# Longer loop bodies and an earlier first front in the two axis stages of a convolution and state-space kernel

## What is computed

```python
def selective_scan(u, delta, A, B, C, D):
    A = jnp.clip(A, -5.0, 5.0)
    dA = jnp.einsum('bld,dn->bldn', delta, A)
    dB_u = jnp.einsum('bld,bld,bln->bldn', delta, u, B)
    c = jnp.concatenate([dA[:, 1:], jnp.zeros_like(dA[:, :1])], axis=1)
    c = jnp.exp(jnp.minimum(jnp.cumsum(jnp.flip(c, axis=1), axis=1), 15.0))
    c = jnp.flip(c, axis=1)
    x = jnp.cumsum(dB_u * c, axis=1) / (c + 1e-06)
    y = jnp.einsum('bldn,bln->bld', x, C)
    return y + u * D

def mamba(x, in_w, conv_w, conv_b, xproj_w, dproj_w, dproj_b, A_log, Dp, out_w):
    ...   # in-projection, 4-tap convolution over the sequence, SiLU
    A = -jnp.exp(jnp.clip(A_log, -5.0, 5.0))
    ...   # delta, B, C from the projection of x1
    y = selective_scan(x1, delta, A, B, C, Dp)
    return y * jax.nn.silu(res) @ out_w.T
```

## Time and profile before

| what | value |
|---|---|
| runs | 19094.44, 19100.8, 19101.3 us |
| the profiled execution, its own time | 19113.85 us |
| span of the profile, first to last instruction | 19112.1 us |
| PE busy | 16120.1 us (84%) |
| VectorE busy | 17478.0 us (91%) |
| ScalarE busy | 13984.3 us (73%) |
| GpSimd busy | 15672.6 us (82%) |
| mean granted TensorE clock | 0.964 |

### The profile page before, as it was taken

How to read it: one execution, slowest core, us unless ns; L and a number is a source line. 1 busy time by engine, 2 the same in 40 slices (tenths; PEclk the granted TensorE clock), 3 DMA queues, 4 the chain that set the end, 5 groups by cost and what they waited for, 6 DMA issues and landing times. The chain is left out here.

```text
span 19112.1 us, 290534 instructions
## 1 busy us (share of the span) xinstructions
PE 16120.1 (84%) x60280; PEld 8249.4 (43%) x60280; DVE 17478.0 (91%) x48304; ACT 13984.3 (73%) x18454; POOL 15672.6 (82%) x10820
## 2 busy tenths in 40 slices
PE   5786888888888888888688888888888888887666
PEld 2333444444444444444344444444444444442222
DVE  3888999999999999999899999999999999996666
ACT  4665777777777777777577777777777777772566
POOL 2665888888888889888699999999999999984555
PEclk8998999999999999999899999999999999998888
DMA  1001000000000000000000000000000000000000
GB/s 33 14 13 14 11 11 10 10 10 11 11 11 11 11 11 11 11 11 11 12 11 11 11 11 11 11 11 11 11 11 11 11 11 11 11 9 22 11 11 10
DMA packets 778298, 228.57 MB, mean 12 GB/s; under 512 B 747760, under 2 KB 750476, under 8 KB 776332
## 3 DMA queue, kind: packets, MB, share of 16 engines
q1 hardware_dynamic: 776332, 206.79, 8.3%
HBM read 143.66 MB, written 62.97 MB: 11 GB/s over the span
## 5 line engine op out<-in xcount | busy, mean ns | idle before, releaser
L1238 POOL TENSOR_TENSOR h_sm<-h_sm,h_wr 128x768 f32<-128x768 f32 x2944 | 5399.7, 1834 | 695.6 <-DVE h_wr L1018 610.2
L1238 POOL TENSOR_TENSOR w_sm<-w_sm,w_wr 128x768 f32<-128x768 f32 x2944 | 5398.5, 1834 | 502.5 <-DVE w_wr L1018 405.0
L1402 PE MATMUL w_pz<-w_xr,w_tri 128*128 128x384 f32 x9984 | 4461.3, 530 | 787.3 <-DVE w_wr L1018 620.9
L1402 PE MATMUL h_pz<-h_xr,h_tri 128*128 128x384 f32 x9984 | 4436.6, 527 | 767.6 <-DVE h_wr L1018 603.5
L1018 DVE SCALAR_TENSOR_TENSOR h_wr<-h_pz,h_bct,h_rbuf 128x192 f32<-128x192 f32 x11776 | 4253.3, 408 | 181.3 <-PE h_pz L1402 180.8
L1018 DVE SCALAR_TENSOR_TENSOR w_wr<-w_pz,w_bct,w_rbuf 128x192 f32<-128x192 f32 x11776 | 4242.2, 408 | 99.2 <-PE w_pz L1402 98.7
L992 DVE SCALAR_TENSOR_TENSOR h_xr<-h_cbuf,h_bct,h_pdx 128x192 f32<-128x192 f32 x9984 | 3635.8, 405 | 73.5 <-issue 32.9
L992 DVE SCALAR_TENSOR_TENSOR w_xr<-w_cbuf,w_bct,w_pdx 128x192 f32<-128x192 f32 x9984 | 3634.5, 405 | 74.1 <-issue 33.1
L1114 ACT ACTIVATE h_cbuf<-h_pe_e,h_consts 128x1024 f32<-128x1024 f32 x2304 | 2525.7, 1112 | 1541.6 <-PE h_pe_e L1390 1341.2
L1114 ACT ACTIVATE w_cbuf<-w_pe_e,w_consts 128x1024 f32<-128x1024 f32 x2304 | 2526.4, 1112 | 1493.9 <-PE w_pe_e L1390 1295.8
L1137 ACT ACTIVATE w_rbuf<-w_pe_e,w_consts 128x1024 f32<-128x1024 f32 x2304 | 2476.3, 1113 | 0.0
(11 more groups left out here) (362 smaller groups left out, 20130.6 us busy)
## 6 DMA issues: line engine op xcount, KB each, us to landing
h_lt<-pieces_s SPq DMA_DIRECT2D x512, 96.0 KB, 4.4
w_lt<-pieces_s SPq DMA_DIRECT2D x512, 96.0 KB, 4.3
pieces_s<-h_pieces SPq DMA_DIRECT2D x384, 48.0 KB, 2.1
pieces_s<-w_pieces SPq DMA_DIRECT2D x384, 48.0 KB, 2.1
h_xt<-first_s SPq DMA_DIRECT2D x34, 128.0 KB, 5.5
w_xt<-first_s SPq DMA_DIRECT2D x34, 128.0 KB, 3.1
m_u<-hn_s SPq DMA_DIRECT2D x32, 128.8 KB, 2.7
m_u<-slots_s SPq DMA_DIRECT2D x32, 128.8 KB, 2.6
```

The source lines that it names most:

```text
L1238: tt(sm[:, g], sm[:, g], wr[:, u % 3], ALU.add).then_inc(s_add, 1)
L1402: t.matmul(pz[:, P % 2, 0:2 * DX], tri[:], x, start=True, stop=True).then_inc(s_z, 1)
```

## The change

Three things change, all in `phase_axis`.

1. The loop's body holds six passes instead of two (`BODY`): 10 turns for passes 1 to 60, and passes 61, 62 and 63 written out.
2. The weight loads are split over two queues: 15 stay on SyncE, 12 are issued by ScalarE. The first input load moves from behind `s_go` to behind the clearing of `xt` (new semaphore `s_pad`), which now is the first of the memsets.
3. `s_go` is given ahead of the pieces of A and the spreading. The clip of A moves to the front of VectorE's preparation (`s_clip`). Of the 16 spreading instructions VectorE issues 7 (3 before the prefix sum, 4 behind it), ScalarE 6 (ahead of its first `c_group`) and GpSimd 3 (behind its third piece); TensorE waits for the three of them (`s_dec`) before the first `fill`.

```diff
+        BODY = 6
+        TURNS = (NT2 - 2) // BODY
@@ bodies
-            with eng.Fori(0, NT2 // 2 - 1) as m:
-                for k in (1, 2):
-                    yield m * 2 + k, k % 2, m + 1, False, False
-            yield NT2 - 1, 1, 0, False, True
+            with eng.Fori(0, TURNS) as m:
+                for k in range(1, BODY + 1):
+                    yield m * BODY + k, k % 2, m * (BODY // 2) + (k + 1) // 2, False, False
+            for T in range(TURNS * BODY + 1, NT2):
+                yield T, T % 2, (T + 1) // 2, False, T == NT2 - 1
@@ sync
+                sp.wait_ge(s_pad, 1)
+                load_x(place(0), 0)
                 sp.wait_ge(s_go, 1)
-                load_x(place(0), 0)
@@ vector
-                for big in (inw, inz, wdt, wbc, wo, xt):
+                v.memset(xt[:], 0.0).then_inc(s_pad, 1)
+                for big in (inw, inz, wdt, wbc, wo):
                     v.memset(big[:], 0.0)
...
                 dve.wait_ge(s_w, 16 * NW)
+                v.tensor_scalar(am, am, -5.0, 5.0, ALU.max, ALU.min).then_inc(s_clip, 1)
...
-                for d in range(16):
-                    last = v.tensor_scalar(decay[:, :, :, d], asel.rearrange("p (m n) -> p m n", n=NX), low4[:, d:d + 1],
-                                           None, ALU.mult)
-                step(last)
                 for m, (s, n) in enumerate([(s_r, 2), (s_wd, 2), (s_add, UN), (s_res, 1), (s_e, 2 * GRP), (s_go, 1)]):
                     v.memset(mark[:, m:m + 1], 0.0).then_inc(s, n)
...
+                a_pieces()
                 make_xc(0, 0)
+                for d in range(3):
+                    make_decay(d)
                 prefix(0)
+                for d in range(3, 7):
+                    last = make_decay(d)
+                last.then_inc(s_dec, 1)
                 make_gate(0, 0)
@@ scalar
+                act.wait_ge(s_asel, 1)
                 piece1(0)
                 piece2(0)
                 sig_z(3)
+                for d in range(10, 16):
+                    last = a.activation(decay[:, :, :, d], asel.rearrange("p (m n) -> p m n", n=NX), ACT.Identity,
+                                        scale=low4[:, d:d + 1])
+                last.then_inc(s_dec, 1)
@@ gpsimd
                 piece3(0)
+                for d in range(7, 10):
+                    last = nc.gpsimd.tensor_scalar(decay[:, :, :, d], asel.rearrange("p (m n) -> p m n", n=NX),
+                                                   low4[:, d:d + 1], None, ALU.mult)
+                last.then_inc(s_dec, 1)
@@ tensor
                 pe.wait_ge(s_lt[0], 128)
+                pe.wait_ge(s_dec, 3)
```

More of the change, by code:

```diff
@@ L769, in phase_axis @@
         s_go, s_xt, s_pd = sem(tag + "prepared"), sem(tag + "input"), sem(tag + "pieces_stored")
+        s_pad, s_clip, s_asel, s_dec = (sem(tag + n) for n in ("input_cleared", "a_clipped", "a_pieces", "decay_made"))
         s_lt = [sem(tag + "pieces_loaded0"), sem(tag + "pieces_loaded1")]
@@ L836, in _ @@
                 ld(ident[:], ident_in)
[L837 to L840, removed]
                 for i in range(8):
@@ L942, in _, with a_pieces, make_decay @@
                 step(v.tensor_tensor(bsc[:, 1:2], bn[:, 1:2], bsc[:, 2:3], ALU.subtract))
[L944 to L954, removed]
-                for d in range(16):
-                    last = v.tensor_scalar(decay[:, :, :, d], asel.rearrange("p (m n) -> p m n", n=NX), low4[:, d:d + 1],
-                                           None, ALU.mult)
-                step(last)
                 for m, (s, n) in enumerate([(s_r, 2), (s_wd, 2), (s_add, UN), (s_res, 1), (s_e, 2 * GRP), (s_go, 1)]):
                     v.memset(mark[:, m:m + 1], 0.0).then_inc(s, n)
+                def a_pieces():
+                    dve.wait_ge(s_aexp, 2)
+                    step(v.tensor_scalar(am, am, 5.0, None, ALU.min))
+                    step(v.tensor_copy(around, am))
+                    v.tensor_scalar(asel, around, pick[:, 0:1], None, ALU.mult)
+                    step(v.tensor_tensor(arest, am, around, ALU.subtract))
+                    step(v.tensor_copy(around, arest))
+                    v.scalar_tensor_tensor(asel, around, pick[:, 1:2], asel, ALU.mult, ALU.add)
+                    step(v.tensor_tensor(arest, arest, around, ALU.subtract))
+                    step(v.tensor_copy(around, arest))
+                    v.scalar_tensor_tensor(asel, around, pick[:, 2:3], asel, ALU.mult, ALU.add).then_inc(s_asel, 1)
+                    dve.wait_ge(s_asel, 1)
+                def make_decay(d):
+                    return v.tensor_scalar(decay[:, :, :, d], asel.rearrange("p (m n) -> p m n", n=NX),
+                                           low4[:, d:d + 1], None, ALU.mult)
                 def make_xc(F, q):
@@ L1054, in _, with ld @@
                 a = nc.scalar
+                def ld(dst, src):
+                    act.dma_start(dst, src).then_inc(s_w, 16)
+                ld(inT, w["inT"])
+                ld(upT, w["upT"])
+                ld(dtT, w["dtT"])
+                ld(taps, w["taps"].rearrange("k (j d) -> k j d", j=JB).partition_broadcast(128))
+                for g in range(2):
+                    q = slice(64 * g, 64 * g + 64)
+                    ld(down2[:, q], w["down"])
+                    ld(outw2[:, :, g, :], w["outw"].rearrange("e (j d) -> e j d", j=JB))
+                    ld(xpr2[:, :, g, :], w["xpr"].rearrange("r (j d) -> r j d", j=JB))
+                    ld(xpT[q], w["xpT"].rearrange("(j d) n -> d j n", j=JB))
                 act.wait_ge(s_prep, 1)
@@ L1059, in _ @@
                 a.activation(bsc[:, 3:4], bsc[:, 3:4], ACT.Exp, scale=-0.5).then_inc(s_aexp, 1)
-                act.wait_ge(s_aexp, 2)
+                act.wait_ge(s_clip, 1)
                 a.activation(am, am, ACT.Exp).then_inc(s_aexp, 1)
```

4 lines of the change are left out of this document (removed).

## The result

The changed kernel takes **18935.2 us** in the median of four runs. Before took 19101.05 us on the same chip. The ratio of the undisturbed runs is 0.9909, with a 95% interval of 0.9895 to 0.9922: 174 us faster (149 to 201). Forecast were 231 us, with a range down to 176: right in direction, and too good by 57 us. The median over all four lies 10 us above the upper end of the range, the mean of the three 2 us above it, and two of the three lie within it; so the range is missed narrowly, the gain clearly.

What follows compares the result with a forecast made beforehand. VectorE was taken to set the pace in the passes, with nearly serial phase heads. Jumps 120.5 us plus heads 110.2 gave 230.7 us off 19100.8, so 18870 us, range 18845 to 18925.

Steps and rivals of the forecast that it cites:

- the head's: Both phase heads: first weight load to `xc` 59.5 and 55.7 us earlier, less 2.5 each for contention; 110.2 us together.
- Jumps: Loop of both phases: 21 fewer jumps back each, at 2.72 us in `h_` and 3.02 in `w_`; 120.5 us saved.
- I cost a join of two written-out passes at nothing: Pass loop: a pass following another without a jump carries no surcharge, as pass 1 behind pass 0; cost zero.
- Weights: Phase head: loads on two queues bring first issue to first use from 16.0 to 11.5 us.
- `s_go` and the pieces: Phase head, from first use of the weights to `xc`: 12.0 us to `s_go`, then 9.5 for VectorE's pieces.
- I take 2.0, nearer to VectorE's 2.47, since the write is the same: hidden by a hair: Phase head: each of ScalarE's six spreading instructions takes 2.0 us, within its 2.26 us of cover, so no delay.
- the upper bound of 3.8: ScalarE's spreading: at most 3.8 us each, 1.16 us times VectorE's ratio 3.25; `fill` then 9.3 us late.
- by length 2.75 us: GpSimd's three spreading instructions: 2.75 us each, scaled from a 1.834 us addition, hidden within 4.8 us each.
- Contention: Phase head: GpSimd and VectorE hinder each other during spreading; 2.5 us a phase taken, between nothing and 9.9.
- the rule of the exclusive lock: Phase head: by the shared port pair, GpSimd's three steps could each wait behind a VectorE instruction, 7.4 us a phase at most.
- The second rival: Phase heads: spreading becomes late and ends the first `fill`; at most 33 us less gain, 18885 to 18903 us; chance 0.15.
- The third rival: Pass loop: written-out passes starve for code, every join costing what a jump costs; 19180 us, slower; chance 0.03.

Runs made afterwards that it cites:

- loop_only: The kernel before with the six-pass loop body alone, its heads the old ones; 19008.81 us, ratio 0.9953.
- chunks30: The changed kernel with spreading by six contiguously writing VectorE instructions instead of 16 strided ones on three engines, and a body of 30 passes; 18861.75 us, ratio 0.9877.
- head_only: The changed kernel with a body of two passes, its heads the new ones; 19023.47 us, ratio 0.996.
- no_act: The changed kernel with ScalarE's six spreading instructions given to VectorE (13 there, 3 on GpSimd); 18954.91 us, ratio 0.9921.
- loop_again: The same text run once more: the kernel before with the six-pass body alone; 19009.19 us.
- the probe: The changed kernel plus 15 instructions per head, each engine alone writing 1152 bf16 elements at steps 1, 2, 4, 8 and 16; 19078.93 us.

## Why the prediction came out wrong

The 57 us fall into two parts. Between the profiled executions 231 were forecast and 203 came: the heads gained 36 us less and the passes 4 less, and the unchanged phases 12 more, which the prediction had not reckoned with. The other 29 us are no term of the sum: before's profiled execution was 13 us slower than its other runs, after's 16 us faster than the mean of its three. So the one term that failed is the head's, by the spreading.

**Jumps, 120.5 us forecast, 116.7 measured: right.** The count (30 to 9), the place and the mechanism are shown by the waits, by loop_only and by chunks30. Within the sum several sizes were off, and they cancel nearly; that 116.7 lies so close to 120.5 is luck in part.
A jump that is left costs 2.04 and 2.02 us in after, not the 2.72 and 3.02 that it was to keep. I had taken the mean over 30 as if each cost the same. Pass by pass, and beside the granted clock, the price falls into three groups. In `w_` after, the eight microseconds from 3 us behind the copy that opens the jump's pass (columns as above), for passes 7, 19 and 37, which take 121.10, 119.66 and 118.82 us instead of 117.57:

```profile
10233.98:10241.98 8.00, 6.49 (x16) 3.44 (x17) 6.02 (x19) 1.59 (x3) 2.95 (x3) 0.57 0.02 5
11651.61:11659.61 8.00, 7.00 (x22) 3.49 (x22) 7.19 (x22) 3.37 (x7) 3.99 (x4) 0.79 0.02 5
13781.40:13789.40 8.00, 6.66 (x24) 3.25 (x25) 7.94 (x25) 4.29 (x8) 4.86 (x5) 1.00 0.02 6
```

The third is the jump alone: 1.25 us more, about VectorE's own 1.1 of the waits, and the clock stays at full. In the second it is at its lower level for a part of the stretch, and the pass is 2.1 us longer; in the first for nearly all of it, 3.5 us. VectorE gets through 19, 22 and 25 instructions. Counted over all jumps (no fall, a short one as in pass 19, a long one as in pass 7), at 1.2 to 1.9, 2.0 to 2.6 and 3.1 to 4.0 us each, but for three that cost more (two in which the clock falls once more later in the pass, and the first of `w_` before, 5.1 us):

| jumps with | no fall | a short one | a long one | mean price |
|---|---|---|---|---|
| before, `h_` | 4 | 8 | 18 | 2.76 |
| before, `w_` | 2 | 14 | 14 | 2.94 |
| after, `h_` | 2 | 7 | 0 | 2.04 |
| after, `w_` | 5 | 2 | 2 | 2.02 |

So in after the clock also falls less behind the jumps that are left. That need not be the longer body's doing: head_only, with the body of two, has only 8 long falls in `h_`, and a mean of 2.51 us. Why a fall is long, short or missing, no run tells.

In `h_` the surcharges of all jumps thus fall by 30 x 2.76 - 9 x 2.04 = 64 us, more than the 57. But "I cost a join of two written-out passes at nothing" was half wrong. Between passes of the body there is no surcharge, while the passes written out outside the loop take 121.4 (pass 0), 121.5 and 121.2 us where those of the body take 119.57. The earlier trace rows showed it in pass 0, and I read it as pass 0's own. The two more that the change writes out cost 3.5 us.

The trace says where it is lost. The timeline of VectorE's prefix sum (L970) and GpSimd's addition (L1263) in pass 60, the last of the loop, and in pass 61:

```profile
8890.46 0.94 DVE L970 TENSOR_TENSOR_SCAN h_sf<-h_mask,h_dt 128x384 f32<-128x384 f32 x1
8890.53 2.50 POOL L1263 TENSOR_TENSOR h_sm<-h_sm,h_wr 128x768 f32<-128x768 f32 x1
...
9010.09 1.81 POOL L1263 TENSOR_TENSOR h_sm<-h_sm,h_wr 128x768 f32<-128x768 f32 x1
9010.27 2.45 DVE L970 TENSOR_TENSOR_SCAN h_sf<-h_mask,h_dt 128x384 f32<-128x384 f32 x1
```

In the loop VectorE starts first, by 0.07 us, and GpSimd's instruction takes 2.50 us instead of 1.81. In pass 61 GpSimd starts first, by 0.18 us, and it is VectorE's that takes longer: 2.45 us instead of 0.94, which is 1.5 of the 1.6 to 1.9 us. That is the pattern of no_act, where the one that comes second waits. All ten traces agree: the prefix sum, some 67 us into the pass, takes 2.4 to 2.5 us in passes 0, 61 and 62 wherever they are written out, and 0.94 to 1.3 us in each pass of a body. No run moved the two apart, so the cause is read from the traces and not tested. What shifts the two engines by 0.25 us against each other is open; in the trace the passes outside have separate semaphore instructions where those of the body have register ones.

In `w_` the clock falls without a jump, too. The copies ahead of passes 3 and 4 after:

```profile
9757.45 0.55 DVE L1003 COPY w_dxs<-w_pdx 128x384 f32<-128x384 f32 x1
9876.66 0.55 DVE L1003 COPY w_dxs<-w_pdx 128x384 f32<-128x384 f32 x1
```

They lie 119.2 us apart, 1.6 more than most. The windows view from 41 us into pass 3 (columns as above), and the same place two passes on:

```profile
9798.00:9800.00 2.00, 1.41 (x4) 0.59 (x4) 2.00 (x7) 2.00 (x3) 1.22 (x2) 1.00 0.00 0
9800.00:9802.00 2.00, 2.00 (x7) 1.17 (x6) 2.00 (x7) 0.33 (x1) 2.00 (x2) 0.64 0.00 0
9802.00:9804.00 2.00, 2.00 (x7) 1.29 (x7) 1.09 (x4) 0.00 (x0) 2.00 (x2) 0.51 0.00 0
10038.00:10040.00 2.00, 2.00 (x10) 1.17 (x11) 2.00 (x7) 0.74 (x1) 1.60 (x1) 1.00 0.00 0
10040.00:10042.00 2.00, 2.00 (x13) 1.45 (x11) 2.00 (x7) 0.62 (x1) 2.00 (x3) 1.00 0.00 0
```

TensorE has been idle for 0.85 us up to 9798.59, in the first window, is then granted 0.64 and 0.51 of its clock, and gets through 7 instructions in each window instead of 10 and 13; in the second of them VectorE waits for its sums. The idle time alone doesn't explain it: TensorE is idle for the same 0.85 us at the same place in every pass of the `w_` loop, also where the clock stays at full. Nine passes of `w_` show this in after (eight in the loop and pass 62), five in before, none of `h_`. Whether they belong to the longer body was a question of loop_only's expectation. Passes of the loop without a jump that show it: 2 and 3 in the traces with a body of two (before, head_only), 7 to 21 in the seven with a body of six (after 8, loop_only 7, loop_again 14), 16 with a body of thirty. So they go with the longer body, though their number varies between executions of one text, and they take back some of its gain; why, no run tells. The eight cost 13 us, the two in before that had no jump 3 us, and the passes outside the loop take 4 us more than in before; so `w_` gained 55.6 us and not the 30 x 2.94 - 9 x 2.02 = 70 of its jumps.

**Weights, 11.5 us forecast, 12.1 and 12.7 measured** (1536.99 to 1549.11 in the lines above). **`s_go` and the pieces, 21.5 us forecast, 21.3 measured** (1549.11 to 1570.42). Right.

**"I take 2.0, nearer to VectorE's 2.47, since the write is the same: hidden by a hair" is the step that failed.** The spreading ended the `fill` in both phases, as the prediction said would show it wrong. ScalarE's instruction costs 4.8 us in a row, above the upper bound of 3.8. That bound carried the ratio of VectorE's strided to its dense write, 3.25, over to ScalarE, and from 1.16 us; the probe has 5.11 / 1.25 = 4.1. GpSimd's, "by length 2.75 us", costs 6.8 alone, since 1.834 us was the price of a dense addition; it would have been late too, had ScalarE not been. Beyond the front's own lateness ScalarE's six cost (1621.00 - 1606.6) = 14.4 us in `h_`, with 1606.6 the time at which `lt` would have let the `fill` go (14.34 us behind the third piece's end at 1592.29, as in the earlier trace rows). So the terms that failed are the two instruction prices: 2.0 us taken for ScalarE, 4.8 measured, and 2.75 taken for GpSimd, 6.5 in a row at best.

**Contention, 2.5 us taken, 5.5 measured**, within the bounds of nothing and 9.9, and each of GpSimd's three steps is behind one of VectorE's, as the rule of the exclusive lock had it (7.4 at most). Together 5.5 - 2.5 + 14.4 = 17.4 us a phase, of the 18.1 and 18.0 that the heads fell short.

**The second rival happened**, with a chance of 0.15 and at most 33 us; it cost some 35. It named the right mechanism and had its upper bound from the same wrong ratio. The range's upper end, 18925, was no sum of its terms: 9 and 33 us lead to 18912, and with the 26 of dearer jumps to 18938. That the profiled execution (18911) still lies in the range is luck: the unchanged phases took 12 us less and the execution was the fastest.

**The third rival** (written-out passes starve) is refuted: with 30 passes in the body, in chunks30, no pass of `h_` but the jump's is longer than 119.6 us, and the 1.6 to 1.9 us of the passes outside the loop lie nearly all in the prefix sum, 67 us behind the join.

## What to carry to other kernels

Where VectorE sets the pace in a loop with a long body, count its waits for "issue" against the number of turns: a jump back cost 1.2 to 4.0 us in most cases here, in step with what TensorE's clock did behind it, and a longer body removes it; look at the single values of such a price before a mean is multiplied. Before an element-wise instruction is handed to another engine, look at the step of its writes: the strided form costs 2 to 4 times the dense one, with another ratio on each engine, so that a bound must not borrow one engine's ratio for the next. An order of loops that writes densely on one engine, and keeps it away from GpSimd's short steps, was worth 20 us a phase more than three engines sharing the strided form. And look at which of two engines that take turns starts first: a shift of 0.25 us decided whether VectorE or GpSimd paid for the meeting.

## What the runs showed of the hardware that I had not expected

- A bf16 write of 1152 elements costs 0.82, 1.25 and 3.20 us densely on VectorE, ScalarE and GpSimd, and 2.78, 5.39 and 7.08 at a step of 8; step 16 costs no more.
- VectorE and GpSimd with this instruction take turns, 8.65 us a pair, and a short GpSimd instruction beside it takes 2.5 to 3.2 instead of 0.8 to 0.9 us.
- A jump back has a price of about 1.3, 2.2 or 3.5 us, in step with how long TensorE's clock is at its lower level behind it (not at all, a short or a long while); and the same nine jumps of the same text cost 2.07 us in the mean of one execution and 4.16 in another, with TensorE idle for 3.0 and 4.4 us. The cause of the latter is open.
- TensorE's clock falls in the middle of some `w_` passes, behind 0.85 us of idle time that all of them have, and that costs 1.6 us; no pass of `h_` shows it. With a body of two 2 or 3 passes of the loop without a jump show it, with longer bodies 7 to 21.
- Passes written out ahead of and behind the loop take 1.6 to 1.9 us more than those in it, where the clock doesn't fall. 1.5 us of it is VectorE's prefix sum, which takes 2.45 us instead of 0.94 when GpSimd's addition starts 0.18 us ahead of it, and not 0.07 us behind.
